# Gate and up products of a mixture layer as seven half-size products per block instead of eight

## The reference, cut to what matters

```python
x = x + tanh(g_xattn) * xattn(layernorm(x), ctx, ...)      # 8 x 256 tokens of 512
x = x + tanh(g_ffn) * ffn(layernorm(x), ...)

def ffn(x):                                # xt: (2048, 512)
    probs = softmax(xt @ w_router)         # 128 experts
    topk_p, topk_idx = top_k(probs, 4)
    topk_w = topk_p / (sum(topk_p) + EPS)
    gate = (xt @ w_gate).reshape(T, 8, 256)
    up = (xt @ w_up).reshape(T, 8, 256)
    basis = silu(gate) * up                # (T, 8, 256)
    mix = p / (sum(p) + EPS)               # p from amplitudes, (128, 8)
    mixed = einsum('tek,tki->tei', mix[topk_idx], basis)
    out = einsum('teh,te->th', mixed @ w_down, topk_w * expert_scale[topk_idx])
    shared = silu(xt @ shared_w_gate) * (xt @ shared_w_up) @ shared_w_down
    return out + shared
```

## Time and profile before

| what | us |
|---|---|
| median of 3 runs (lowest, highest) | 1025.92 (1025.29, 1026.58) |
| the profiled execution, its own time | 1024.73 |
| its span, first to last instruction | 1022.9 |
| PE busy | 966.8 (95%) |
| DVE busy | 466.5 (46%) |
| ACT busy | 336.6 (33%) |
| POOL busy | 175.2 (17%) |

### The profile page before, as it was taken

How to read it: one execution, slowest core, us unless ns; L and a number is a source line. 1 busy time by engine, 2 the same in 40 slices (tenths; PEclk the granted TensorE clock), 3 DMA queues, 4 the chain that set the end, 5 groups by cost and what they waited for, 6 DMA issues and landing times.

```text
span 1022.9 us, 17783 instructions
## 1 busy us (share of the span) xinstructions
PE 966.8 (95%) x7128; PEld 831.7 (81%) x7128; DVE 466.5 (46%) x1023; ACT 336.6 (33%) x714; POOL 175.2 (17%) x213
## 2 busy tenths in 40 slices
PE   6689999999999999989989979999999999999998
PEld 6678989898888889877867866888888888888887
DVE  5356574747566575753224654322222222223245
ACT  5655444444444444546113222111111111111121
POOL 2020000101000000011001200002334433334330
PEclk9979999999999999999999989999999999999999
DMA  6585566566656555893042000401101110110003
GB/s 215 169 217 136 132 157 154 144 181 157 176 146 163 136 143 132 223 249 115 4 162 83 21 0 3 142 23 62 52 32 62 42 62 21 62 62 22 20 18 147
DMA packets 74706, 108.61 MB, mean 106 GB/s; under 512 B 5497, under 2 KB 48250, under 8 KB 73594
## 3 DMA queue, kind: packets, MB, share of 16 engines
...
## 4 chain that ended last, share of the span: by engine, by line
PE 86%; DVE 6%; DMA 3%; issue 2%; ACT 2%; SPq 1%; POOL 0%; ACTq 0%; DVEq 0%
PE ps_scores L1197 23%; PE ps_proj L1197 21%; PE ps_scoresT L1197 21%; PE ps_o L1310 5%; PE ps_scoresT L1297 4%; PE ps_scores L1276 4%; PE ps_o_max L1321 2%; DMA xn_rows<-in_x 1%; DVE neg_max L928 1%; DMA q_kept<-qT_hi 1%; PE ps_proj L1220 1%; DVE actT_lo L893 1%; DMA q_stack<-max_rows 1%; PE ps_o L1197 1%; DVE x_normal L974 1%
## 5 line engine op out<-in xcount | busy, mean ns | idle before, releaser
L928 DVE TENSOR_REDUCE neg_max<-ps_scores 128x2 f32<-128x384 f32 (+1 forms) x256 | 130.5, 517 | 126.5 <-PE ps_scores L1276 125.5
L679 ACT ACTIVATE probsT<-ps_scoresT 128x512 f32<-128x512 f32 (+1 forms) x256 | 138.8, 544 | 141.1 <-PE ps_scoresT L1297 137.7
L715 ACT ACTIVATE silu_gate<-ps_scores 128x512 f32<-128x512 f32 x80 | 47.8, 598 | 362.9 <-PE ps_scores L1197 362.9
L986 DVE TENSOR_TENSOR basis<-ps_scoresT,silu_gate 128x512 f32<-128x512 f32 x64 | 44.3, 692 | 244.0 <-PE ps_scoresT L1197 244.0
L1197 PE MATMUL ps_scores<-xnT_hi,w_hi 128*128 128x512 f32 x320 | 125.1, 391 | 2.3 <-POOL w_lo L580 1.6
L1197 PE MATMUL ps_scores<-xnT_lo,w_hi 128*128 128x512 f32 x320 | 124.6, 389 | 0.0
L1197 PE MATMUL ps_scores<-xnT_hi,w_lo 128*128 128x512 f32 x320 | 124.5, 389 | 0.0
L1197 PE MATMUL ps_scoresT<-xnT_lo,w_hi 128*128 128x512 f32 x320 | 124.5, 389 | 0.0
L1197 PE MATMUL ps_scoresT<-xnT_hi,w_hi 128*128 128x512 f32 x320 | 124.5, 389 | 0.0
L1197 PE MATMUL ps_scoresT<-xnT_hi,w_lo 128*128 128x512 f32 x320 | 124.5, 389 | 0.0
L1276 PE MATMUL ps_scores<-k_stack,q_stack 114*128 114x192 f32 (+1 forms) x512 | 104.0, 288 | 9.0 <-DVE neg_max L928 7.2
...
## 6 DMA issues: line engine op xcount, KB each, us to landing
...
k_kept<-kT_hi SPq DMA_DIRECT2D x16, 256.0 KB
...
```

The lines of the kernel that those rows point to most:

```text
L679: act.activation(PT[:, g % 2, 2 * j:2 * j + blocks].rearrange("p h f r w -> p (h f r w)"), ST[:, n % 2, 0:blocks].rearrange("p h n -> p (h ...
L715: act.activation(SG[:, q % 2, :], PG[:, q % 2, :], ACT.Silu).then_inc(silu_done, 1)
L928: dve.tensor_reduce(NM[:, g % 2, 2 * i:2 * i + 2], SA[:, n % 2, :, 0:keys], AX.X, ALU.max, negate=True).then_inc(max_done, 1)
L986: return dve.tensor_tensor(dst, PU[:, q % 2, :], SG[:, q % 2, :], ALU.mult).then_inc(prod_done, 1)
```

## The change

The inputs of a gate or up product are split in two halves of 256 (two chunks each), the tokens in two halves (groups 0, 1 and groups 2, 3), and the outputs are gate and up. That is a product of 2 x 2 blocks. Winograd's form of Strassen's method does it with seven block products and 15 block sums. A **unit** is one feature block with token groups g and g + 2. The 32 units (u = 2n + g) each have seven parts of 6 matmuls (2 chunks by 3 passes), 42 instead of 48.

- **PE** issues per unit: 1(u), 4(u-1), 2(u), 3(u-1), 6(u), 5(u), 7(u). Parts 1, 6, 7, 4 add onto one `ps_scores` bank, 5 and 3 onto one `ps_scoresT` bank, 2 uses `ps_proj`. ACT copies the running sum out after parts 1, 6 and 7 (`take`), and parts 6, 7 and 4 wait for those copies.
- **Token sums.** s2 and s3 (4 blocks of 128x512 each) are made by POOL during shared gate and up, s1 by POOL during shared down, s4 by DVE from token tile 13 of shared down on. Each is then split: high part on ACT, low part on POOL (s4: DVE). s1 overwrites the chunks of `xnT` that it came from.
- **Weight sums.** Per feature block POOL makes four sums of 128x256 (`weight_sums`), ACT seven high parts and POOL seven low parts of 128x256, in place of two each of 128x512.
- **DVE** per unit: three additions of a PSUM bank to a copy in SBUF (`gate_first`, `up_second`, `up_first`), two products with the silu, two with the coefficients. Before, per two tiles, two and two. POOL still adds twice.
- **x.** The place of `x_rows` is taken. In shared down each row tile comes through four buffers (`x_part`) and goes back to DRAM, and for the down products it comes again (`x_last`): 5 tiles early, 11 once part 7 of the last unit is done.
- **Order at the end.** Pairs go 4, 5, 0, 1, 6, 7, 2, 3. Pair 4 is multiplied after part 7 of unit 31, then part 4, pair 5, part 3, and the others.

```diff
@@ -49,6 +49,25 @@
+MEETS = {B11: "a11", B21: "a12", B22: "s4", T1: "s1", T2: "s2", T3: "s3", T4: "a22"}
+UNITS_E = 2 * NE
...
+PAIR_ORDER = (4, 5, 0, 1, 6, 7, 2, 3)
...
+W_ORDER = (B11, B21, T1, T2, T3, B22, T4)
+SUMS_AT = {8: 0, 10: 1, 12: 2, 14: 3}
...
@@ -352,8 +392,34 @@
...
+    def operand(name, h, c, g):
+        if name in ("a11", "a12"):
+            return XT[h][:, c + HH * (name == "a12"), group_columns(g)]
+        if name in ("a21", "a22", "s1"):
+            return XT[h][:, c + HH * (name == "a22"), group_columns(g + 2)]
+        return SUM[int(name[1])][h][:, c, group_columns(g)]
...
@@ -524,23 +587,53 @@
...
+        def load_part(t):
+            if t < 4:
+                sp.wait_ge(prod_done, NS * NG)
+            else:
+                sp.wait_ge(xb_kept[t % 4], 16 * (t // 4))
+            sp.dma_start(XB[t % 4][:], x1_rows[:, t]).then_inc(xb_in[t % 4], 16)
+        for t in range(4):
+            load_part(t)
+        for t in range(NT):
+            sp.wait_ge(sd_out, t + 1)
+            sp.dma_start(x1_rows[:, t], XB[t % 4][:]).then_inc(xb_kept[t % 4], 16)
+            if 1 <= t <= NT - 4:
+                load_part(t + 3)
...
+        for i in range(4):
+            sp.wait_ge(xb_kept[i], 64)
+        for i, t in enumerate(TILE_ORDER):
+            if i == 0:
+                sp.wait_ge(part_mm, multiplied(3, 2 * LAST - 1))
+            if i == 3:
+                sp.wait_ge(e_lo, 7 * NE)
+            if i == EARLY:
+                sp.wait_ge(part_mm, multiplied(7, UNITS_E - 1))
+            sp.dma_start(XF[i][:], x1_rows[:, t]).then_inc(xf_in[i // 2], 16)
+        for i, t in enumerate(TILE_ORDER):
+            sp.wait_ge(d_out, i + 1)
...
@@ -605,25 +698,120 @@
...
+        def difference(i):
...
+            link(pool.tensor_tensor(s3, v("a11", "hi"), v("a21", "hi"), ALU.subtract))
+            link(pool.tensor_tensor(s2, v("a11", "lo"), v("a21", "lo"), ALU.subtract))
+            pool.tensor_tensor(s3, s3, s2, ALU.add).then_inc(s_raw, 1)
+            pool.wait_ge(s_raw, 2 * i + 1)
+            link(pool.tensor_tensor(s2, v("a22", "hi"), v("a22", "lo"), ALU.add))
+            pool.tensor_tensor(s2, s2, s3, ALU.subtract).then_inc(s_raw, 1)
...
+        def weight_sums(n):
...
+            link(pool.tensor_tensor(t1, quarter(n, 0, 1), quarter(n, 0, 0), ALU.subtract))
+            link(pool.tensor_tensor(t2, quarter(n, 1, 1), t1, ALU.subtract))
+            link(pool.tensor_tensor(t3, quarter(n, 1, 1), quarter(n, 0, 1), ALU.subtract))
+            pool.tensor_tensor(t4, quarter(n, 1, 0), t2, ALU.subtract).then_inc(t_sums, 1)
...
+        def add_up(u):
...
+            for j, t in enumerate((g + 2, g)):
+                pool.wait_ge(basis_done, 2 * u + j + 1)
+                dst = mixed[:, n % HALF, group_columns(t)]
+                pool.tensor_tensor(dst, dst, BS[:, j, :], ALU.add).then_inc(acc_done, 1)
...
+        pool.wait_ge(router_mm, NG)
+        split_lo(SHARED + 2)
+        difference(0)
+        difference(1)
+        sum_low("s3", 0)
+        sum_low("s2", 0)
+        split_lo(SHARED + 3)
...
+        split_lo(SDOWN)
+        split_lo(SDOWN + 1)
+        sum_low("s3", 3)
+        sum_low("s2", 3)
+        total(0)
...
+        weight_sums(0)
+        weight_low(0, W_ORDER)
+        weight_sums(1)
+        for u in range(UNITS_E):
+            n, g = divmod(u, 2)
+            if n < LAST:
+                weight_low(n + 1, W_ORDER[4 * g:4 + 3 * g])
+                if g == 1 and n + 2 < NE:
+                    weight_sums(n + 2)
+            elif g == 0:
+                split_lo(DOWN)
+            if u >= 1:
+                add_up(u - 1)
+        add_up(UNITS_E - 1)
...
@@ -806,12 +1010,13 @@
...
-            if q == 12:
+            if q in SUMS_AT:
+                sum_high("s3", SUMS_AT[q])
+                sum_high("s2", SUMS_AT[q])
+            if q == 13:
                 split_hi(SDOWN)
-            if q == 13:
...
@@ -837,29 +1042,76 @@
...
+            if t in (3, 5, 7, 9):
+                sum_high("s1", (t - 3) // 2)
+            if t == 12:
...
+                weight_high(0, W_ORDER)
+            if t >= 14:
+                sum4_high(t - 14)
...
+        def take(u, part, src, j):
...
+            act.wait_ge(part_mm, multiplied(part, u))
+            act.activation(TP[:, u % 2, j, :], src[:, u % 2, :], ACT.Copy).then_inc(taken, 1)
...
+        for u in range(UNITS_E):
+            n, g = divmod(u, 2)
+            if u >= 2:
+                act.wait_ge(e_prod, 2 * (u - 1))
...
+            take(u, 1, PG, 0)
+            if u >= 1:
+                second_silu(u - 1)
+            if n < LAST:
...
+                weight_high(n + 1, W_ORDER[4 * g:4 + 3 * g])
+            elif g == 0:
+                split_hi(DOWN, (part_mm, multiplied(3, 2 * LAST - 1)))
+            act.wait_ge(c11_done, u + 1)
+            act.activation(TP[:, u % 2, 0, :], TP[:, u % 2, 0, :], ACT.Silu).then_inc(g1_silu, 1)
+            take(u, 6, PG, 1)
...
+            if u == UNITS_E - 1:
+                pair_hi(0)
+                pair_hi(1)
+            take(u, 7, PG, 2)
+        second_silu(UNITS_E - 1)
...
@@ -1133,58 +1385,124 @@
...
+        def sum4(i):
...
+            link(dve.tensor_tensor(dst, operand("a12", "hi", c, g).bitcast(F32), operand("a12", "lo", c, g).bitcast(F32),
+                                   ALU.add))
+            link(dve.tensor_tensor(other, operand("s2", "hi", c, g).bitcast(F32), operand("s2", "lo", c, g).bitcast(F32),
+                                   ALU.add))
+            dve.tensor_tensor(dst, dst, other, ALU.subtract).then_inc(s4_raw, 1)
+            dve.wait_ge(s4_raw, i + 1)
...
         for t in range(NT):
             if t >= 2:
-                add_rows(t - 2, PJ[:, t % 2, :], sd_mm, sd_out)
+                add_shared(t - 2)
             shared_lo(t)
+            if t >= 13:
+                sum4(t - 13)
...
-            add_rows(t, PJ[:, t % 2, :], sd_mm, sd_out)
...
+            add_shared(t)
+        sum4(3)
+        for i in range(len(BLOCKS)):
+            sum4_low(i)
+        def gate_first(u):
...
+            dve.tensor_tensor(TP[:, u % 2, 0, :], TP[:, u % 2, 0, :], PJ[:, u % 2, :], ALU.add).then_inc(c11_done, 1)
+        def up_second(u):
...
+            dve.tensor_tensor(TP[:, u % 2, 2, :], TP[:, u % 2, 2, :], PU[:, u % 2, :], ALU.add).then_inc(c22_done, 1)
+        def up_first(u):
...
+            dve.tensor_tensor(TP[:, u % 2, 1, :], TP[:, u % 2, 1, :], PU[:, u % 2, :], ALU.add).then_inc(c12_done, 1)
+        def times_up(u, j):
...
+                silu, up = SG[:, u % 2, :], TP[:, u % 2, 2, :]
+            else:
...
+                silu, up = TP[:, u % 2, 0, :], TP[:, u % 2, 1, :]
+            dve.tensor_tensor(BS[:, j, :], up, silu, ALU.mult).then_inc(e_prod, 1)
...
+        for u in range(UNITS_E):
+            if u >= 1:
+                up_second(u - 1)
+                times_up(u - 1, 0)
+            gate_first(u)
+            if u >= 1:
+                basis(u - 1, 0)
+                up_first(u - 1)
+                times_up(u - 1, 1)
+                basis(u - 1, 1)
+        u = UNITS_E - 1
+        pair_lo(0)
+        up_second(u)
+        pair_lo(1)
+        times_up(u, 0)
+        basis(u, 0)
+        add_pair(0)
+        up_first(u)
+        times_up(u, 1)
+        basis(u, 1)
+        for i in range(2, PAIRS):
+            pair_lo(i)
+            add_pair(i - 1)
+        add_pair(PAIRS - 1)
...
@@ -1504,25 +1822,69 @@
...
+        def part(number, u, bank, w, first):
...
+            n, g = divmod(u, 2)
+            for c in range(HH):
+                for j, (s, m) in enumerate(PASSES):
+                    ins = pe.matmul(bank[:, u % 2, :], WS[n % 2][s][:, w, c * P:(c + 1) * P], operand(MEETS[w], m, c, g),
+                                    start=first and c == 0 and j == 0, stop=c == HH - 1 and j == PARTS - 1,
...
+        pe.wait_ge(sd_out, NT)
+        for u in range(UNITS_E):
+            pe.wait_ge(e_lo, 7 * (u // 2 + 1))
+            if u >= 2:
+                pe.wait_ge(g2_silu, u - 1)
+            part(1, u, PG, B11, True)
...
+                part4(u - 1)
+            if u >= 2:
+                pe.wait_ge(c11_done, u - 1)
+            part(2, u, PJ, B21, True)
...
+                part3(u - 1)
...
+            pe.wait_ge(taken, 3 * u + 1)
+            part(6, u, PG, T2, False)
...
+            part(5, u, PU, T1, True)
+            pe.wait_ge(taken, 3 * u + 2)
+            part(7, u, PG, T3, False)
+        u = UNITS_E - 1
+        pe.wait_ge(w_lo, 2 * EXPERT + 2)
+        pair_down(0)
+        part4(u)
+        pe.wait_ge(c11_done, UNITS_E)
+        pair_down(1)
+        part3(u)
+        for i in range(2, PAIRS):
+            pair_down(i)
```

344 lines of the change are left out of this document (234 added, 110 removed).

## The result

| what | before | after |
|---|---|---|
| median (lowest, highest), us | 1026.25 (1025.29, 1028.14), 4 runs | 998.93 (993.87, 1003.41), 4 runs |
| ratio of the two, 95% interval | | 0.973 (0.968 to 0.978) |
| the profiled execution, its own time, us | 1024.73 | 1003.41 |
| its span, us | 1022.9 | 1001.6 |

The forecast was 999.5 us, in 990 to 1014. One execution each of `thin_parts`, `filler`, `best_filled` and of the kernel before beside the last of them took 1.5 to 3.1 times as long as the rest (slow runs) and is left out of every median and comparison here.

What follows compares the result with a forecast made beforehand. From 650 us on TensorE alone was taken to bound the kernel. 1024.7 - 43.5 + 2 + 4.2 + 3.0 + 4.9 + 3.4 = 998.7 us for the profiled execution; with the median 1.2 us higher, 999.5 us was forecast, range 990 to 1014.

Steps and rivals of the forecast that it cites:

- 192 matmuls: Experts: 1536 matmuls become 1344, at 0.2267 us each; 43.5 us less, 9.52 us per unit in place of 10.88.
- steady state: Expert units: other engines keep up with PE; zero added, with 0.4 us per unit (13 us) as the other end.
- to shared down: Shared gate and up: more POOL instructions, taking turns with DVE, and DVE's coefficients held up; +2 us (0 to 4).
- waits at the end of shared down: Tiles 13 to 15: PE idle before tiles 14 and 15, then waiting for the last addition; +4.2 us (2.5 to 7).
- first unit: First expert unit: ACT's first copy, and part 6 with it, wait behind DVE's s4 work; +3.0 us (2 to 5).
- tail, first pair: Unit 31: DVE's low part for the first pair done at 10.6 to 11.8 us, PE wants it at 9.52; 1.7 us.
- tail, third pair: After part 3 of the last unit: the third pair's low part stands behind `up_first` on DVE; 3.2 us.
- clock: Half clock on PE after added waits, around shared down's end and in the tail, 1.7 us each; +3.4 us (0 to 7).
- attention: Attention stage, before shared gate and up: the prediction's sum has no term for it.
- Rival 1: Every expert unit: DVE or ACT late by 0.15 to 0.5 us; 1004 to 1016 us, middle 1009; chance 0.22.
- sum of turns: Expert units: DVE and POOL instructions that take turns add up to 8.8 us of 9.52; it fits.
- rival 2: Kernel end bound by DMA: 256 KB loads at 0.2 MB per us; 8 us more, 1007 us; chance 0.08.

Runs made afterwards that it cites:

- thin_parts: Changed kernel with five of the six matmuls of parts 2 and 5 left out in every unit (sums incomplete); 966.19 us, ratio to before 0.939.
- filler: Changed kernel with 17 and 8 matmuls that nobody reads in PE's two waits ahead of shared down; 993.89 us, ratio to before 0.969.
- best_filled: The `combined` kernel with 13 and 8 matmuls that nobody reads in PE's two waits ahead of shared down; 984.74 us, ratio to before 0.961.
- experiment 1: Changed kernel with six matmuls that nobody reads behind part 7 of every unit; 1041.84 us, ratio to before 1.016.
- again: The changed kernel run once more with nothing changed; 1003.57 us, ratio to before 0.975.
- experiment 2: Three variants of the changed kernel: `thin_parts`, 966.19 us; unread POOL additions in 26 units, one of 128x256, 998.58 us, or two of 128x512, 1033.69 us.
- early_sums: Changed kernel with POOL making the first two blocks of s2 and s3 before the third shared weight pair's low parts; 999.09 us, ratio to before 0.972.
- combined: Changed kernel with `early_sums`, s4 blocks later, the tail's third-pair low part earlier, and POOL pausing after the low parts of w_down; 990.01 us, ratio to before 0.963.

## Why the prediction was right, step by step

| step | forecast | measured |
|---|---|---|
| 192 matmuls | -43.5 | -43.5 (9.52 us a unit, and experiment 1) |
| steady state | 0 (0 to 13) | 0 |
| to shared down | +2 (0 to 4) | +1.9 |
| waits at the end of shared down | +4.2 (2.5 to 7) | +3.1; +4.5 in `again` |
| first unit | +3.0 (2 to 5) | +2.1 |
| tail, first pair | +1.7 | 0 |
| tail, third pair | +3.2 | +3.0 |
| clock | +3.4 (0 to 7) | +6.2 in the profile of after, about +1.0 in `again` |
| attention | 0 | +3.8 in the profile of after |

The right column (profile of after) adds up to 23.4 us less, and the spans differ by 21.3. Of the 2 us between them 0.4 are a wait for `down_lo` at 618.98, which the forecast didn't have; the rest isn't broken down.

- **Main term and steady state.** As forecast. Rival 1 (small stalls in every unit) is out: no wait between 667 and 976 us. The turns are real, but the unit has room for them; experiment 2 puts the bound at 8.5 us where the sum of turns had 8.8.
- **Way to shared down.** +1.9 us, as forecast, by one of the two paths named: POOL's low parts of `w_down` were done at 601.99, 1.9 us before PE's first product (603.91), and DVE's coefficients, held up by POOL, set the time (`early_sums` and `combined`).
- **Shared down.** The wait before tile 14 (1.97 us, forecast 2.0) and before the first expert product (1.11, forecast 1.1) came out, that before tile 15 hardly did: of the 4.6 us on `down_lo` 2.25 lie ahead of shared down and 1.97 before tile 14. Tile 14 ran at half clock, and so came late by itself. In `again` it ran at full clock, and there the wait came, with 1.39 us. Wait and half clock cover each other, so the two terms may not both be added in full.
- **First unit.** Part 6 waited 2.14 us for ACT's copy behind s4. I had 4.8 + 0.7 us against 2.7. The fourth block took 2.2 us and the four low parts 2.50, nearly as forecast (2.2 and 2.6), but the block began at 661.33, 0.34 us ahead of the unit's first product.
- **Tail.** The step that failed is the first pair. The product with the coefficients of unit 30 was to end 9.9 us into unit 31 and ended at 966.47, 8.3 us in; the low part followed at once and was ready at 967.07, before PE wanted it at 967.70:

```profile
964.71 1.03 DVE L1460 TENSOR_TENSOR basis<-part_sums 128x512 f32<-128x512 f32 x1
...
966.39 0.68 DVE L1479 TENSOR_TENSOR down_lo<-big,down_hi 128x512 fp32r<-128x512 f32 x1
```

The forecast gives no steps for its 9.9 us, only "with POOL adding beside it"; in these last steps DVE lost 0.34 us to POOL, once (1.03 in place of 0.69). The third pair's 3.2 us came as 3.00.
- **Clock.** That half clock follows the added waits was right for the profile of after, with three places and not two (tile 14, first unit, tail), of 7, 8 and 13 long steps, and a stretch 3 steps longer at the start of shared down: 6.2 us in place of 3.4. In `again` only the tail had one, so this term is a matter of chance from one execution to the next. The errors of the tail (1.9 too much) and of the clock (2.8 too little) work against each other, which is why the sum looks better than its parts.
- **DMA (rival 2).** Not seen. `x_last` and its stores are behind nobody; the last addition ends at 999.17 and the span at 1001.6, 2.4 us later, as before (1020.49 and 1022.9). The issues with count, KB and median us to landing answer to the earlier trace rows:

```profile
x_part<-x_kept SPq DMA_DIRECT2D x16, 256.0 KB, 2.9
...
x_last<-x_kept SPq DMA_DIRECT2D x16, 256.0 KB, 4.5
out<-x_last SPq DMA_DIRECT2D x16, 256.0 KB, 2.0
```

- **The median.** That 999.5 met 998.93 is in part luck. The profiled execution was 4.5 us over the median, and 3.8 us of its time came from attention. The forecast took 2 us as what a measurement of this kernel can tell; its four runs lie 9.5 us apart, and a second series of the same kernel has its median at 1003.57.
